# Regrouping the routing stage of a GNN, mixer and expert kernel: scales for two tiles at a time, scatters in pairs, another order on VectorE and TensorE, and padding rows written from SBUF

## The reference

```
xn = layernorm(x)
x  = x + gnn(xn) + mixer(xn)          # two SAGE convolutions, a linear attention mixer
z  = layernorm(x)                     # the expert layer
logits = z @ Wr + br                  # 8 experts, each row goes to its best one (top 1)
x  = x + gate * (relu(z @ W1[e] + b1[e]) @ W2[e] + b2[e])      # e = the row's expert
```

## Time and profile before

| what | value |
|---|---|
| time, median of 3 runs | 2641.74 us (2640.11 to 2643.08) |
| the profiled execution | 2644.86 us, span 2642.9 us |
| mean granted TensorE clock | 0.967 of full speed |
| PE, DVE, ACT, POOL busy | 92%, 67%, 42%, 45% |
| routing stage, first L1227 to last L1264 | 2126.4 to 2355.96 us |
| first tile load of the experts issued | 2372.1 us |

### The profile page before, as it was taken

How to read it: one execution, slowest core, us unless ns; L and a number is a source line. 1 busy time by engine, 2 the same in 40 slices (tenths; PEclk the granted TensorE clock), 3 DMA queues, 4 the chain that set the end, 5 groups by cost and what they waited for, 6 DMA issues and landing times.

```text
span 2642.9 us, 39517 instructions
## 1 busy us (share of the span) xinstructions
PE 2436.1 (92%) x11512; PEld 1931.0 (73%) x11513; DVE 1777.5 (67%) x3701; ACT 1116.8 (42%) x2055; POOL 1186.0 (45%) x1092
## 2 busy tenths in 40 slices
PE   5999999999999998999999899899999957759897
PEld 4788888888888886888888566677777745547675
DVE  5677777767877763444344477788878567747887
ACT  3455455444444443444334323233333245535554
POOL 5576777666666660000000045555555435542333
PEclk8999999999999999999999999999999979879999
DMA  9866656455555545544444467788888687745554
GB/s 371 250 174 187 195 159 190 120 151 142 125 149 129 140 115 185 224 170 168 188 191 176 153 190 212 219 233 240 228 226 237 157 345 292 280 144 185 182 180 140
DMA packets 159400, 511.55 MB, mean 194 GB/s; under 512 B 30354, under 2 KB 30866, under 8 KB 126658
## 3 DMA queue, kind: packets, MB, share of 16 engines
q1 hardware_dynamic: 110020, 381.71, 40.8%
q0 software_dynamic: 49280, 128.61, 22.1%
HBM read 268.06 MB, written 244.32 MB: 194 GB/s over the span
## 4 chain that ended last, share of the span: by engine, by line
PE 80%; DMA 8%; DVE 5%; issue 3%; POOL 2%; ACT 1%; SPq 1%; DVEq 0%; POOLq 0%; ACTq 0%
PE bank L1363 53%; PE bank L1414 8%; PE bank L1370 5%; DMA agg_d<-O,eidx 4%; PE bank L1614 4%; PE bank L1478 2%; PE bank L1547 1%; PE bank L453 1%; PE bank L454 1%; PE bank L1617 1%; POOL r_rows L809 1%; DMA a_x<-in_x 1%; DVE r_rows L1227 1%; DVE pd L1192 1%; DVE st L1230 1%
## 5 line engine op out<-in xcount | busy, mean ns | idle before, releaser
L414 POOL DMA_INDIRECT agg_d<-O,eidx x160 | 274.4, 1715 | 221.2 <-DMA agg_d<-O,eidx 163.2
L350 POOL TENSOR_TENSOR G_low<-G,G_high 128x512 fp32r<-128x512 f32 x160 | 237.9, 1487 | 227.9 <-ACT G_high L475 227.5
L397 POOL DMA_INDIRECT G<-y_d,esrc x80 | 85.2, 1065 | 527.2 <-DMA y_d<-b_y 514.3
L433 DVE SCALAR_TENSOR_TENSOR Sj<-erow,dstf,tri 128x128 f32<-128x128 int32 x160 | 190.1, 1188 | 30.7 <-DMA agg_d<-O,eidx 30.6
L475 ACT CAST G_high<-G 128x512 fp32r<-128x512 f32 x160 | 99.2, 620 | 180.7 <-DVE G L1077 172.8
L820 POOL DMA_INDIRECT out<-x_out,x_id x88 | 84.4, 959 | 188.8 <-DVE x_out L1318 184.7
L442 DVE SCALAR_TENSOR_TENSOR eidx<-cnt,todump,dstf 128x1 int32<-128x1 f32 x160 | 149.1, 932 | 7.6
L948 ACT CAST qz_high<-low 128x512 fp32r<-128x512 f32 x80 | 49.6, 620 | 235.2 <-PE bank L1363 135.6
L774 POOL TENSOR_TENSOR pd<-pd,low 128x512 f32<-128x512 f32 (+1 forms) x80 | 142.1, 1776 | 0.0
L350 POOL TENSOR_TENSOR a_xn_rows_low<-a_x,a_xn_rows_high 128x512 fp32r<-128x512 f32 x80 | 141.6, 1771 | 0.3 <-ACT a_xn_rows_high L846 0.3
L1363 PE MATMUL bank<-Wk_high,xnT_high 128*128 128x512 f32 x320 | 127.8, 399 | 6.3 <-DVE xnT_low L350 6.3
(11 more groups left out here) (227 smaller groups left out, 7512.9 us busy)
## 6 DMA issues: line engine op xcount, KB each, us to landing
x_rows<-xs_d SPq DMA_DIRECT2D x88, 260.0 KB, 2.7
agg_d<-zero SPq DMA_DIRECT2D x20, 1040.0 KB, 20.2
b_agg<-agg_d SPq DMA_DIRECT2D x20, 1040.0 KB, 8.8
a_x<-in_x SPq DMA_DIRECT2D x20, 1024.0 KB, 7.3
agg_d<-z_halves SPq DMA_DIRECT2D x20, 1024.0 KB, 5.9
q_d<-q_rows SPq DMA_DIRECT2D x80, 256.0 KB, 2.4
r_d<-r_rows SPq DMA_DIRECT2D x80, 256.0 KB, 3.8
r_in<-r_d SPq DMA_DIRECT2D x20, 1024.0 KB, 6.8
```

The lines of the kernel that those rows point to most:

```text
L350: return eng.tensor_tensor(out_, full, high.bitcast(F32), ALU.subtract)
L397: pool.indirect_dma_start(G[:, j, :], None, table, bass.IndirectOffsetOnAxis(ap=esrc[:, b, j:j + 1], axis=0)).then_inc(e_g[j], 16)
L414: pool.indirect_dma_start(agg, bass.IndirectOffsetOnAxis(ap=eidx[:, j, 0:1], axis=0), O[:, j, 0:width], None, compute_op=ALU.add).then_inc ...
L433: dve.scalar_tensor_tensor(Sj[:, :], row, dstf[:, b, j:j + 1], tri[:, :], ALU.is_equal, ALU.mult, accum_out=cnt[:, j:j + 1]).then_inc(e_cn ...
```

## The change

Five edits, all in the routing stage and the hand-over:

1. GpSimd makes the scales in two halves of two tiles. A turn is now: two scatters, scales of tiles 0 and 1 (waiting for `x2(1)` only), two scatters, scales of tiles 2 and 3. ScalarE's `normal(0)` and `normal(2)` wait for the half they need.
2. TensorE does `rank()` behind `turn_row(0)`.
3. VectorE does `places()` behind `x2(3)`.
4. The padding rows are loaded once into SBUF (`x_pad`) and written from there. This load and the two W1x loads stand behind group 17's loads (W1x was behind group 3's).
5. The copy into the end of W1x stands behind step 18 of the table.

```
 SP   if isinstance(g, int) and g == 3:      ->   g == 17:
+         sp.dma_start(pad[:, :], pad_in).then_inc(r_pad, 16)
          ... two loads into W1x
-     sp.dma_start(xs_d[bass.ds(end, P), :], pad_in).then_inc(r_pad, 16)
+     sp.dma_start(xs_d[bass.ds(end, P), :], pad[:, :]).then_inc(r_pad, 16)

 POOL route
+    for half in range(2):
+        two = slice(2 * half, 2 * half + 2)
+        if active(g, 3, NG):
+            if half == 0:
+                need_apart(pool, r_ch, CH * (g - 2))
+            for j in range(2 * half, 2 * half + 2):
+                pool.indirect_dma_start(xs_d.ap(), ... place[:, k3, j, 0:1] ..., rows[:, k3, j, :], None)
+        if active(g, 0, NG):
+            need_apart(pool, r_x2, 13 * g + 7 + 6 * half)
+            pool.tensor_scalar(veps[:, two], rows[:, k, two, D + 1], EPS, None, ALU.add)
+            pool.tensor_scalar(rows[:, k, two, D + 2], rows[:, k, two, D], -1.0, None, ALU.mult)
+            pool.tensor_tensor(rows[:, k, two, D + 1], veps[:, two], nhalf[:, two], ALU.pow)
+            pool.tensor_tensor(rows[:, k, two, D + 2], rows[:, k, two, D + 2], rows[:, k, two, D + 1], ALU.mult)

 ACT  normal(j)
-    if j == 0:      act.wait_ge(r_v, 3 * g)
+    if j % 2 == 0:  act.wait_ge(r_v, 6 * g - 3 + 3 * (j // 2))

 DVE  x2(2)
+     x2(3)
      if active(g, 2, NG):
          places()
-     x2(3)
      ...
      (the copy into W1x's end: from ahead of made(1) to ahead of made(19))

 PE   turn_row(0)
+     rank()
      turn_row(1)
      logits(0)
      turn_row(2)
-     rank()
      logits(1)
```

More of the change, by code:

```diff
@@ L211, in build @@
                                enumerate(("equal", "score", "onehot", "place")))
-        lgT = at("r_logitsT", 9.125, shape=[P, 2, GROUP])
+        lgT, pad = at("r_logitsT", 9.125, shape=[P, 2, GROUP]), at("x_pad", 9.625, shape=[P, AW])
         mx, td, te, rt, m2, pf = (word(f"r_{n}", 1408 + 8 * i, [TG]) for i, n in
@@ L702, in route @@
                     agg_in(g, k)
-                if isinstance(g, int) and g == 3:
+                if isinstance(g, int) and g == 17:
+                    sp.dma_start(pad[:, :], pad_in).then_inc(r_pad, 16)
                     for n in range(2):
@@ L711, in _ @@
             quad_turns(sp, route, 0, last=1)
+            sp.wait_ge(r_pad, 16)
             sp.wait_ge(r_tb, 1)
@@ L716, in _ @@
                 end = sp.value_load(runi[0:1, e:e + 1], min_val=0, max_val=EXP * REG - P)
-                sp.dma_start(xs_d[bass.ds(end, P), :], pad_in).then_inc(r_pad, 16)
+                sp.dma_start(xs_d[bass.ds(end, P), :], pad[:, :]).then_inc(r_pad, 16)
             for k in range(4):
                 sp.wait_ge(r_sc[k], 16 * NT // 4)
-            sp.wait_ge(r_pad, 16 * EXP)
+            sp.wait_ge(r_pad, 16 * (EXP + 1))
             sp.wait_ge(r_tb, TB)
@@ L797, in route @@
                 g = 4 * turn + k
[L798 to L812, removed]
+                k3 = (k - 3) % 4
@@ new lines, in route @@
+                for half in range(2):
[4 more added lines that the diff above has]
+                        for j in range(2 * half, 2 * half + 2):
+                            pool.indirect_dma_start(xs_d.ap(),
+                                                    bass.IndirectOffsetOnAxis(ap=place[:, k3, j, 0:1], axis=0),
+                                                    rows[:, k3, j, :], None).then_inc(r_sc[k3], 16)
+                    if active(g, 0, NG):
+                        need_apart(pool, r_x2, 13 * g + 7 + 6 * half)
+                        pool.tensor_scalar(veps[:, two], rows[:, k, two, D + 1], EPS, None, ALU.add)
+                        pool.tensor_scalar(rows[:, k, two, D + 2], rows[:, k, two, D], -1.0, None, ALU.mult
+                                           ).then_inc(r_v, 1)
+                        pool.wait_ge(r_v, 6 * g + 3 * half + 1)
+                        pool.tensor_tensor(rows[:, k, two, D + 1], veps[:, two], nhalf[:, two], ALU.pow
+                                           ).then_inc(r_v, 1)
+                        pool.wait_ge(r_v, 6 * g + 3 * half + 2)
+                        pool.tensor_tensor(rows[:, k, two, D + 2], rows[:, k, two, D + 2], rows[:, k, two, D + 1],
+                                           ALU.mult).then_inc(r_v, 1)
@@ L974, in normal @@
                     i = 4 * (g - 1) + j
-                    if j == 0:
-                        act.wait_ge(r_v, 3 * g)
+                    if j % 2 == 0:
+                        act.wait_ge(r_v, 6 * g - 3 + 3 * (j // 2))
                     need(act, r_tr, i - 1)
@@ L1283, in _ @@
             dve.wait_ge(r_ch, CH * NG)
-            dve.tensor_copy(W1x[:, EXP * KC * P:].rearrange("p (a n) -> p a n", a=3),
-                            cst[:, None, 0:P].to_broadcast([P, 3, P]))
             made(1, dve.tensor_copy(runi[one, :], run[one, :]))
@@ L1305, in _ @@
             made(18, dve.tensor_copy(tabE[one, :], tabf[one, 0, :]))
+            dve.tensor_copy(W1x[:, EXP * KC * P:].rearrange("p (a n) -> p a n", a=3),
+                            cst[:, None, 0:P].to_broadcast([P, 3, P]))
             made(19, dve.tensor_scalar(tabS[one, :], tabf[one, 1, :], run[one, EXP - 1:EXP], None, ALU.min))
@@ L1580, in route @@
                     turn_row(0)
+                if active(g, 2, NG):
+                    rank()
+                if active(g, 1, NG):
                     turn_row(1)
@@ L1583, in route @@
                     turn_row(2)
-                if active(g, 2, NG):
-                    rank()
-                if active(g, 1, NG):
                     logits(1)
```

## The result

The changed kernel took 2654.91 us (median of 20 runs, 2643.92 to 2685.48), the kernel before 2647.57 us beside it (20 runs, 2634.98 to 2655.59): ratio 1.0034, 95% interval 1.0022 to 1.0046. One disturbed run, the 2685.48, isn't in the ratio. So the sign of the difference isn't settled, and what holds both times is that the forecast gain didn't come. The profiled execution took 2654.52 us.

A forecast was written before the change was run, and what follows sets the result against it. A ring of waits, no full engine, bounds routing. Turns +1.9, start -4.4, end of routing -1.5, copy -0.5 and padding -3.2 give -7.7 us: median 2641.7 to 2634.0, range 2619 to 2649.

The forecast's parts named there:

- TensorE's ring: Routing turn, from best through rank, three tiles and logits to the next best: 9.0 to 9.2 us, far end 15.
- scatter ring: Routing turn, x2(0) waiting for the previous scatters: 7.4 us plus landing time, taken as 10.35 us and the bound.
- rival 2: Routing: the matmul ring becomes the bound at low clock, 11.3 us a turn, +15, 2649; chance 0.18 together with rival 1.
- L: Landing time of scatter 4 in the scatter ring: taken nearest to 2.7 us; 3.8 among a group's loads, 7.8 among W2a's.
- rival 1: Routing: scatter 4 falls among loads, L 3.8 to 4.2, turn 11.3 us, 2649; chance 0.18 together with rival 2.
- W2a and W1x: Weight loads in routing: scatter waits lengthen turns 13 and 14, together 6.2 to 10.2 us, taken as 8.
- The turns together: Turns 3 to 19 of routing: 165.6 plus 8 plus 5 for low clock, 178.6 against 176.7 us, +1.9.
- The start: Start of routing, turn 2: VectorE's waits for first logits and rank shrink, -4.4 us of 4.66.
- The end of routing: Last first tile to last places: 24.5 us after against 26.3 before, taken as -1.5 us.
- The copy of W1x's end: Hand-over: the copy no longer delays the first table step by 0.55 us; -0.5 us.
- The padding: Hand-over: eight padding writes from SBUF, 1.1 us apart instead of 1.46, last landing sooner; -3.2 us, bounds 0 and -4.
- The halves' price in GpSimd's work: GpSimd in routing: product meeting VectorE's combining costs +0.2 us a turn, 3 us in 16, held inside 10.35.

The follow-up runs named there:

- c3: Changed kernel with a group's loads issued 1.9 us later and eight filler matmuls at the end of each TensorE turn: 2644.94 us, ratio 0.9953.
- a4: Changed kernel with unused filler matmuls on TensorE, eight at the turn's end and three ahead of rank: 2678.50 us, ratio 1.0070.
- b1: Changed kernel with rank behind turn_row(2), W1x and padding loads behind group 3's, and a group's loads issued 1.9 us later: 2634.06 us, ratio 0.9903.
- c1: Changed kernel with a group's loads issued 1.9 us later, nothing else: 2651.83 us, ratio 0.9979.
- a2: Changed kernel with the W1x and padding loads back behind group 3's loads: 2660.05 us, ratio 0.9995.
- a1: Changed kernel with rank back in its old place behind turn_row(2): 2679.16 us, ratio 1.0075.
- a3: Changed kernel with rank back behind turn_row(2) and the W1x and padding loads back behind group 3's: 2676.27 us, ratio 1.0072.
- b3: Kernel before with only the halves of scales and scatters added: 2664.33 us, ratio 1.0018.

## Why the prediction was wrong

**The step that failed: "TensorE's ring ... 9.0 to 9.2 us".** Its count is right at full clock (9.27 in the changed turn, 9.2 to 9.3 in c3 less the fillers' 0.9). But I priced it at full clock, kept 15 as its far end, and put the low clock into the sum as 5 us for all turns. The ring measured 10.84 in quiet turns and 12.5 in others, which is above the 10.35 of the scatter ring that I took as the bound. The place of rank closes this ring: best waits for a chain that holds three of the four tiles and starts with the best before it, so each microsecond lost in that chain is lost in the turn. And in each plain turn TensorE ran 3 to 7 us at 1.2 GHz, most of it in that chain. I had written that idle time per turn stays about 3 us; that was my argument against rival 2, and it was the wrong thing to look at: TensorE's idle time fell, from 11.7 to 7.0 in 50 us, and so did the clock, from 0.90 to 0.77. What counts is whether the matmuls that run at the low clock are on the ring. The earlier trace rows already showed 0.90. Rival 2 came true, with 11.3 us a turn: the twelve turns without weight loads measured 136.7 us, 11.4 each (that the number is so near is luck, since "less hidden waits" had no row behind it). a4 and c3 raise the clock, and their undisturbed turns shorten at once. That it takes the early rank is shown by b1 against c1, both with later loads: with rank back r_max waits 7.5 us in 5 turns instead of 29.9 in 15, and the ratio is 0.9903 instead of 0.9979 (W1x also differs, and the chip; a2 shows that W1x's place changes neither r_max's waits, 28.9 us in 13 turns, nor those for scatters). a1 can't show it, as its turns of 14 us leave time for any TensorE ring.

Rival 2 also said why the clock falls: TensorE's pause ahead of rank. That isn't shown, and by itself it can't be the reason. In c3 the pause is 0.72 us, longer than the 0.56 here, with full clock behind it, and the kernel before had pauses of 1.10 and 1.57 us in one turn, with full clock up to the turn's end (compare 2244.63 and 2247.56 in the earlier trace rows):

```profile
2242.33 1.29 PE L1370 MATMUL bank<-ident,r_xn 128*128 128x128 f32 x8 [1.57 <-ACT r_xn L978]
```

What the traces show is that in the changed kernel's plain turns the clock fell 0.4 to 1.8 us behind rank's start, and that work in the other pause, at the turn's end, brought most of it back.

**The scatter ring.** L = 2.7 was right for the changed kernel, and its 7.4 us of other terms are not far off: b1's quick turns are 9.2 to 9.7, its others 10.4 to 12.8, and 15.8 at the weights. But "the loads of a group are issued ... about 7 us into the turn, as scatter 4 starts at 7.3; they still have to start up" was wrong. With scatter and loads that close (a1) L is 7, not 2.7, and not the 3.8 of rival 1. It came out right only because TensorE's ring held the loads back. Had my own price for TensorE's ring been met, the kernel would have been slower still, as a1, a3 and a4 show. The decision point of rival 1, L above 3.3, holds: all three are slower.

**W2a and W1x**: 8 us forecast on top of four plain turns. The four turns took 54.1 us, 12.7 more than four of my 10.35, but 8.5 more than four of the 11.4 that plain turns really took. The size was right, the way wasn't: I had two long waits in turns 13 and 14, and there were three, in turns 14 to 16 (14.7 us in all, 15.4 with a short fourth; part of them stands where r_max would have waited), the last of them by the collision of scatter and loads, as c1 shows. a2 shows that the new place of W1x isn't their cause: with W1x back the three waits were 16.3.

**The turns together**: +1.9 forecast, +14.1 measured. Against the forecast 178.6 the twelve plain turns are +8.7 (136.7 against 12 x 10.35 and three quarters of the 5), the four weight turns +3.5 (54.1, r_max at 2266.41 to 2320.53, against 50.65).

**The start**: -4.4 forecast, -4.9 measured. Right. **The end of routing**: -1.5 forecast, +4.7 measured. The last two turns are TensorE's ring and nothing else, and r_max waits for it:

```profile
2354.30 0.19 DVE L1245 TENSOR_REDUCE r_max<-bank 128x4 f32<-128x32 f32 x1 [5.08 <-PE bank L1563]
...
2364.78 0.19 DVE L1245 TENSOR_REDUCE r_max<-bank 128x4 f32<-128x32 f32 x1 [7.33 <-PE bank L1563]
```

That ring is 10.48 here where I had 9.05.

**The copy of W1x's end**: -0.5 forecast; the first table step now starts right behind places (2367.97, places' last at 2367.77 for 0.17 us), and the first padding write comes 1.43 us behind that last one, 1.84 before. Right. **The padding**: the eight writes and the first tile load behind them, on SP:

```profile
L719 SPq DMA_DIRECT2D xs_d<-x_pad x8: 332/332/351, 2369.2 to 2378.4; - x8
```

```profile
xs_d<-x_pad SPq DMA_DIRECT2D x8, 260.0 KB, 2.5
```

They start 1.32 us apart (9.2 us in seven steps), 1.46 before, where 1.1 was forecast. From the first write to the first tile load it is 12.15 us, 14.48 before: -2.3 of the -3.2. Smaller, but of the right kind.

**The halves' price in GpSimd's work**: the power on two columns took 0.72 as taken from the earlier trace rows. The contention for the product came, at half of the 0.2 us a turn (ns min/median/max):

```profile
L819 POOL TENSOR_TENSOR r_rows<-r_rows x40: 197/198/751, 2129.7 to 2349.9; 128x2 f32<-128x2 f32 x40
```

The 21 of turns 3 to 18 that met no combining of VectorE, or at most 0.2 us of one, took 0.20 us; the other 11 took 0.25 to 0.75, the longer the more of a combining they met. Over 0.20 each that is 1.5 us in 16 turns. The Trainium skill (GPSIMD Engine Reference, Key points) says that GpSimd shares its SBUF interfaces with VectorE and contends with its instructions of two SBUF inputs: the trace agrees. It cost the kernel nothing here, since GpSimd wasn't on the ring that set the turn. (Two sums of the prediction are off by little: four scatters at 1.3 are 5.2, not 5.3, and the terms of TensorE's ring add up to 8.8 to 9.2.)

On the queues, a1 bears on the page as the W2a row did. The Trainium skill (DMA: Bandwidth & Descriptors, Queues, rings and completion order) says that an engine takes a packet from each queue in turn, which by my reading would let a small scatter through beside the loads. The runs show 7.3 us from its start to x2(0) beside loads and 2.9 without. The measurement decides; how the engines share the time between them within those 7 us no run here shows.

**What stays open.** Why the same kernel before got 0.90 in one profile and 0.83 in another isn't known; the time differs, and the chip may. The changed kernel showed 0.79, 0.78 and, with later loads, 0.79: it hardly varies, while the kernel before does. Why the clock falls in each turn of the changed kernel, with less idle time than before, is open too. A version of b1 with fillers wasn't run, and neither was the changed kernel with the pause ahead of rank alone filled.

## What to carry to other kernels

Before moving a wait on TensorE, list the matmuls behind it up to the next wait of the ring, price the ring with part of them at half the clock, and see whether it then sets the turn; mean idle time says nothing about that (less idle time, lower clock here). When one ring is shortened, look at what its slowness kept apart: here a scatter and the next loads, 2 us where 1 was enough, worth 4 us a turn. Try the cheap cure first, a later wait ahead of the loads: with rank in its old place it took the kernel from 1.0072 to 0.9903. And measure a difference of a third of a per cent a second time, on another chip, before calling it faster or slower.

## What the runs showed of the hardware

A scatter of 260 KB by GpSimd took 2.7 us with no loads issued for 2 us behind it, and held its waiter 7.3 us when 2 MB of SP's loads were issued 0.24 us behind its start (a1). With the loads 1.0 to 1.15 us behind it, it released its waiter after 3.0 to 3.2 us (b3).

In the changed kernel's plain turns TensorE's clock fell to 1.2 GHz 0.4 to 1.8 us behind rank's start, for 3 to 7 us. Neither one pause of 0.7 us (c3) nor two of 1.10 and 1.57 us (the kernel before, one turn) had to bring that about. Added work without use (16 fp32 instructions, 2.05 us a turn) raised the granted clock from 0.79 to 0.94 and made routing 10.8 us shorter in the profiles, 6.9 us between the medians.

A product of 128x2 on GpSimd took 0.20 us alone and up to 0.75 us beside a combining instruction of VectorE; one of 128x4 in the kernel before 0.20 and up to 0.77.

A DMA of 260 KB out of SBUF instead of DRAM took SP 332 ns to issue instead of 537, and landed in 2.5 us (median) instead of 4.0.
